# Projecting q and k of an attention and mixture-of-experts layer in three float32r products instead of one float32 product

## Reference: what is computed

```python
qkv = x @ W_qkv                      # (16, 1024, 256) @ (256, 768)
q, k, v = jnp.split(qkv, 3, axis=-1) # 16 heads of 16 each
q, k = _rope(q, k)
att = jnp.einsum('bhtd,bhsd->bhts', q, k) / math.sqrt(DH) + mask
y = jnp.einsum('bhts,bhsd->bhtd', softmax(att), v)
x = layernorm(x + y @ W_o)
x = layernorm(x + mixture_of_experts(x))
```

## Time and profile before

| what | value |
|---|---|
| median of 3 runs | 2942.26 us (2939.76 to 3778.07) |
| the profiled execution, its own time | 2941.85 us |
| span of its trace | 2940.1 us |
| PE busy | 2800.5 us, 95% |
| DVE busy | 2651.2 us, 90% |
| ACT busy | 1782.9 us, 61% |
| GpSimd busy | 1061.1 us, 36% |
| one turn of `mid` | 176.1 us, 14 of them |

### The profile page before, as it was taken

The page is one execution under the profiler, slowest core; times in us unless marked ns, Lnnn a source line. Parts: engine busy times, 40 slices in busy tenths (PEclk is TensorE's granted clock), DMA queues, the critical chain, the costliest instruction groups (busy, mean ns, idle before and its releaser), DMA issues. The chain is left out here.

```text
span 2940.1 us, 58492 instructions
## 1 busy us (share of the span) xinstructions
PE 2800.5 (95%) x18752; PEld 1425.7 (48%) x18752; DVE 2651.2 (90%) x8449; ACT 1782.9 (61%) x4125; POOL 1061.1 (36%) x1295
## 2 busy tenths in 40 slices
PE   5899999999999999999999999999999999999987
PEld 2234545545455554545554455554545555455545
DVE  7899999999999999999899999999999999998855
ACT  1466565666756666575666766666575666756650
POOL 3254333343433434334343423434333343423110
PEclk8799999999999999999999999999999999999998
DMA  3112021120212112021110212112021110212000
GB/s 128 35 49 76 20 80 34 46 58 27 77 34 66 37 41 73 20 81 34 50 54 30 73 34 72 31 41 73 20 81 37 50 51 30 77 30 59 2 30 15
DMA packets 136930, 143.84 MB, mean 49 GB/s; under 512 B 29080, under 2 KB 111280, under 8 KB 136368
## 3 DMA queue, kind: packets, MB, share of 16 engines
q1 hardware_dynamic: 135168, 135.88, 15.3%
q10 hardware_dynamic: 1456, 4.23, 0.4%
HBM read 88.11 MB, written 50.33 MB: 47 GB/s over the span
## 5 line engine op out<-in xcount | busy, mean ns | idle before, releaser
L848 ACT ACTIVATE weights<-bank 128x512 f32<-128x512 f32 (+3 forms) x3072 | 1286.5, 496 | 687.0 <-PE bank L1205 679.0
L977 DVE CUSTOM_DVE_ANT_0 bank<-bank,far_q 128x384 f32<-128x384 f32 (+3 forms) x2048 | 949.6, 520 | 70.0 <-PE bank L1189 56.9
L980 DVE TENSOR_REDUCE maxima<-bank 128x1 f32<-128x512 f32 x1024 | 643.1, 683 | 6.7 <-PE bank L1189 4.7
L1227 PE MATMUL attend<-weights,values 128*32 128x512 f32 (+3 forms) x6144 | 635.6, 499 | 7.4 <-POOL weights L767 5.8
L767 POOL TENSOR_SCALAR_AFFINE_SELECT weights<-weights 128x512 f32<-128x512 f32 x512 | 323.8, 639 | 872.2 <-ACT weights L848 869.9
L1189 PE MATMUL bank<-k_stack,q_stack 48*128 48x512 f16 (+3 forms) x3072 | 511.6, 333 | 41.3 <-DVE maxima L977 12.3
L1205 PE MATMUL bank<-q_stack,k_stack 51*128 51x512 f16 (+3 forms) x3072 | 495.3, 330 | 8.6 <-DMA q_stack<-lowrows 5.4
L1189 PEld LDWEIGHTS bank<-k_stack,q_stack 48*128 48x128 f16 x3072 | 164.0, 94 | 458.8 <-issue 143.7
L1129 PE MATMUL bank<-wexp_hi,zT_hi 128*128 128x512 f32 x1024 | 341.0, 414 | 0.9 <-DVE maxima L977 0.2
L1205 PEld LDWEIGHTS bank<-q_stack,k_stack 51*128 51x128 f16 x3072 | 156.9, 94 | 376.4 <-issue 165.6
L1129 PE MATMUL bank<-wexp_lo,zT_hi 128*128 128x512 f32 x1024 | 319.3, 393 | 0.0
(11 more groups left out here) (115 smaller groups left out, 2909.4 us busy)
## 6 DMA issues: line engine op xcount, KB each, us to landing
parts_scratch<-parts SPq DMA_DIRECT2D x128, 256.0 KB, 2.1
q_stack<-parts_scratch SPq DMA_DIRECT2D x384, 64.0 KB, 2.2
k_stack<-parts_scratch SPq DMA_DIRECT2D x384, 64.0 KB, 2.2
x_in<-in_x SPq DMA_DIRECT2D x64, 256.0 KB, 3.0
z<-in_x SPq DMA_DIRECT2D x32, 512.0 KB, 4.3
out<-z SPq DMA_DIRECT2D x32, 512.0 KB, 2.9
q_stack<-lowrows SPq DMA_DIRECT2D x384, 4.0 KB, 1.7
z<-in_w_exp ACTq DMA_DIRECT2D x1, 1024.0 KB, 4.9
```

Source lines behind the costliest of these rows:

```text
L848: act.activation(weights[:, n % NW, hh, c0:CH], bk[bank(c.seg, step)][:, c0:CH], ACT.Exp, scale=DH ** -0.5).then_inc(S["weights_ready"], 1)
L977: dve.tensor_tensor_reduce(out=b[:, 0:w], in0=b[:, 0:w], in1=far_q[:, CH - w:CH], scale=1.0, scalar=-SENTINEL, op0=ALU.add, op1=ALU.max, a ...
L980: dve.tensor_reduce(dst, b[:, 0:w], AX.X, ALU.max).then_inc(fr, 1)
L1227: last = pe.matmul(pv[32 * j:32 * j + 32, c0:CH], values[:, (s + 1) % SLOTS, o:o + 32], weights[:, n % NW, j, c0:CH], start=kb == 0, stop= ...
```

## The change

`XT` gives three tiles instead of one. ACT copies the bank twice, to `xT` as before and to `xT_hi` in float32r, and raises `x_hi_ready`. DVE then takes the bank less `xT_hi` into `xT_lo` and frees the bank. `QK` waits for both `XT` of its 512 tokens to be freed and runs six float32r matmuls with `split_matmul`, as `MOE` does. Before the first step DVE splits the q and k columns of `wqkv` into `wqk_hi` and `wqk_lo`. The tables and banks stay as they are; each `XT` in them now has a part on DVE.

```diff
+        xT_hi = sb("xT_hi", [P, KT, T], F32R)
+        xT_lo = sb("xT_lo", [P, KT, T], F32R)
+        wqk_hi = sb("wqk_hi", [P, KT, 2 * D], F32R)
+        wqk_lo = sb("wqk_lo", [P, KT, 2 * D], F32R)
...
                 if kind == "XT":
                     (j,) = a
                     filled(act, c, step)
-                    act.activation(xT[:, :, 2 * P * j:2 * P * (j + 1)], b[:, :].rearrange("p (k n) -> p k n", k=KT),
-                                   ACT.Copy).then_inc(fr, 1)
+                    tokens = slice(2 * P * j, 2 * P * (j + 1))
+                    act.activation(xT[:, :, tokens], b[:, :].rearrange("p (k n) -> p k n", k=KT), ACT.Copy)
+                    act.activation(xT_hi[:, :, tokens], b[:, :].rearrange("p (k n) -> p k n", k=KT), ACT.Copy) \
+                       .then_inc(S["x_hi_ready"], 1)
...
             dve.wait_ge(S["w_loaded"], W_LOADS * DMA)
+            dve.tensor_copy(wqk_hi[:, :, :], wqkv[:, :, 0:2 * D]).then_inc(S["wqk_split"], 1)
+            dve.wait_ge(S["wqk_split"], 1)
+            dve.tensor_tensor(wqk_lo[:, :, :], wqkv[:, :, 0:2 * D], wqk_hi[:, :, :].bitcast(F32), ALU.subtract) \
+               .then_inc(S["wqk_split"], 1)
...
-                if kind == "B":
+                if kind == "XT":
+                    (j,) = a
+                    tokens = slice(2 * P * j, 2 * P * (j + 1))
+                    dve.wait_ge(S["x_hi_ready"], c.at("x_hi_ready", step))
+                    dve.tensor_tensor(xT_lo[:, :, tokens], b[:, :].rearrange("p (k n) -> p k n", k=KT),
+                                      xT_hi[:, :, tokens].bitcast(F32), ALU.subtract).then_inc(fr, 1)
+                elif kind == "B":
...
                     if c.seg == "pre" and (s, k) == (0, 0):
                         pe.wait_ge(S["w_loaded"], W_LOADS * DMA)
+                        pe.wait_ge(S["wqk_split"], 2)
+                    emptied(pe, c, ("XT", 2 * ch))
                     emptied(pe, c, ("XT", 2 * ch + 1))
                     room()
                     col = which * D + s * P
-                    for kt in range(KT):
-                        last = pe.matmul(b[:, :], wqkv[:, kt, col:col + P], xT[:, kt, ch * CH:(ch + 1) * CH],
-                                         start=kt == 0, stop=kt == KT - 1)
-                    last.then_inc(fu, 1)
+                    split_matmul(b[:, :], lambda i, kt: (wqk_hi, wqk_lo)[i][:, kt, col:col + P],
+                                 lambda j, kt: (xT_hi, xT_lo)[j][:, kt, ch * CH:(ch + 1) * CH]).then_inc(fu, 1)
```

More of the change, by code:

```diff
@@ L364 @@
     "values_copied": ("VCOPY",), "maxima_ready": ("MC",),
-    "averaged": ("N2",), "rooted": ("R1", "R2"), "normed": ("N1A", "N2A"), "hi_ready": ("ZT",),
+    "averaged": ("N2",), "rooted": ("R1", "R2"), "normed": ("N1A", "N2A"), "hi_ready": ("ZT",), "x_hi_ready": ("XT",),
     "shifted": ("GA",), "gate_exp": ("GA",), "gates_ready": ("GB",),
@@ L583, in attention_moe_kernel @@
         names = [*COUNTED, "link", "parts_ready", "turning", "sines", "sp_waits", "pool_waits", "dve_waits",
-                 "zeroed", "zeroed_v", "stepped", "bias_zeroed", "bias_split", "const_v", "const_p", "ident_ready", "w_loaded", "we_loaded", "hi_split", "w_split"]
+                 "zeroed", "zeroed_v", "stepped", "bias_zeroed", "bias_split", "const_v", "const_p", "ident_ready", "w_loaded", "we_loaded", "hi_split", "w_split", "wqk_split"]
         names += [f"{n}{i}" for n in ("stack", "maxrow") for i in range(SLOTS)]
```

## The result

The changed kernel takes 3013.89 us (median of 4 runs, 3009.77 to 3019.13), the kernel before 2942.48 us beside it: a ratio of 1.0244, with a 95% interval from 1.0229 to 1.026. One execution of the kernel before took 3778.07 us and is a slow one; the ratio goes by the fast ones alone. The change makes the kernel 2.4% slower, 72 us. The forecast was 2998 us, within a range of 2955 to 3020.

A forecast was written before the change was run, and what follows sets the result against it. DVE was taken to bound the kernel where XT stands. A turn costs 2.4 + 1.5 - 0.35 = 3.55 us; 15 of these give 53, with the start 56, added to 2941.85: 2998 us, 1.9% slower, range 2955 to 3020.

The forecast's parts named there:

- DVE sets the pace, QK's saving is mostly without effect: From 1117 to 1182 us of a turn PE follows DVE; QK's 43.5 us saving on PE counts only behind QK.0.3.
- The credit behind QK.0.3: Where DVE idles for PE behind QK.0.3, the shorter QK gains 0.35 us a turn, bounds 0 and 0.40.
- Four subtractions, 2.4 us a turn: DVE's new work at the four XT steps: 0.60 us each, bounds 0.60 and 0.68, 2.4 us a turn.
- DVE's wait for ACT, 1.5 us a turn: At XT, DVE waits until ACT has made both copies: 1.5 us a turn, bounds 0 and 2.7.
- QK.0.0 and HT.0.0 wait for the held banks: PE waits there for the subtractions, but DVE has several finished banks before it by then: cost nothing.
- I expect no change from the clock in the turns: The granted clock, 1.00 in all four stretches of the turn read, was expected to stay at the 2.4 GHz level.
- ACT is hidden: Four more ACT copies at 0.48 us, 1.9 us a turn, cost nothing beyond DVE's wait for them.
- The start, 3 us: Before the turns, the weight split delays XT.0's subtraction, holding its bank and a token load: 3 us, bounds 0 and 5.6.
- the first QK is a little shorter: At the start, the first QK step was expected to be a little shorter; no size of its own given.
- PE as the bound: Rival: QK's saving counts in full and DVE's work is hidden, 2901 us, 1.4% faster; chance 0.08.
- The delay hidden: Rival: DVE's 5.8 us a turn of waits for PE take up the delay, leaving only the start, 2945 us; chance 0.09.
- ACT late: Rival: an exponential precedes ACT's copies at two of four waits, 4.55 us a turn, 3013 us, 2.4% slower; chance 0.11.

The follow-up runs named there:

- the last run: Against the changed kernel, three matmuls ahead of PE's waits are repeated in the turns, 11 more matmuls a turn, to keep PE busy: 2999.08 us, ratio 1.0193.

## Why the prediction was right, and where it was not

The time lay in the range and the direction was the likelier of the two, for most of the reasons given. But a change within 2% was held likelier (0.59) than one slower by more (0.39), and the latter came: the forecast of 2998 was 16 us short.

In the profiled executions the span grew by 68.0 us, where 56 were forecast. Thirteen turns took 58.6 us more (46.2 forecast). The time ahead of them grew by 2.9 us (6.6 forecast) and that behind the last XT.0 by 6.5 (419.6 in place of 413.1; 3.6 forecast), and these two nearly cancel. So the 12 us that the forecast lacks there stand in the turns, 180.5 us in the mean, and they are one step. The median lies 4 us above the profiled execution, in executions of which there is no trace.

*DVE sets the pace, QK's saving is mostly without effect.* Right. With QK in float32 the loss is 9 us more, not 42. The credit behind QK.0.3 was put at 0.35 us a turn; 9 / 15 would be 0.6, but the traces show 0.2 to 0.3 at that place (DVE's wait of 0.19 us, and four reductions in 2.59 us in place of 2.47).

*Four subtractions, 2.4 us a turn.* Right: they run 0.60 us from start to start where two stand together, and doing them twice costs at least as much again.

*DVE's wait for ACT, 1.5 us a turn.* Right in kind and place, a little too high: 1.1 us in the trace, 1.2 by the turns of the kernel with later subtractions. XT.1 came without a wait. The 0.06 us that the working adds for the semaphore stood on no row; in the trace after, the subtraction starts 0.03 us behind ACT's copy (1145.22 + 0.62, then 1145.87).

*QK.0.0 and HT.0.0 wait for the held banks, "so I cost that at nothing".* Right for DVE at an even clock: the turns with a clock of 1.00 cost 3.5 us, the forecast's 3.55, with PE's waits in them. That the two agree so well is partly luck: DVE waits 0.4 us less for ACT than forecast, and a small operation named below takes 0.4 us more.

*"I expect no change from the clock in the turns".* This is the step that failed. I read 1.00 in all four stretches before and took it to stay, while the same text forecast more idle time of PE ahead of XT.1, QK.0.0 and HT.0.0. Behind PE's new gaps the clock fell in ten of thirteen turns. Nine of these are 1.2 us longer than the turns without a fall and one 1.9, together 12.7 us: the 12 us that the profiled execution took beyond the forecast. In the medians the last run got 15 us back.

*ACT is hidden.* Right in the changed kernel; without DVE's part its fourth copy ahead of HT.0.0 shows.

*The start, 3 us.* The mechanism came as described, and then was given back. On the way in, XT.2 of the first sequence went on at 21.84 us (19.06 in the earlier trace rows; forecast 22.3):

```profile
18.30 1.29 DVE L981 TENSOR_TENSOR xT_lo<-bank,xT_hi 128x512 fp32r<-128x512 f32 x2
19.01 0.97 SPq L667 DMA_DIRECT2D x_in<-in_x  x2
21.84 1.97 PE L1173 MATMUL bank<-ident,x_in 128*128 128x128 f32 x8 [13.72 <-DMA x_in<-in_x]
...
26.01 0.74 DVE L1025 STREAM_SHUFFLE rope_swap<-bank 128x512 f32<-128x512 f32 x1
```

The first rotation is late by 2.5 us. Yet ACT's copy of XT.0 in the first segment starts at 126.88, not later than before (127.17). With QK in float32 again that copy is at 129.63, and the 2.5 us stay. So the six matmuls take them back, but by which way is open: their steps are shorter ("the first QK is a little shorter" was one of eight), and with them the clock, low from 45 to 50 us on in all three, also rises earlier. From 104 to 114 us (PE busy, clock, DMA), before, after, and after with QK in float32:

```profile
104.00:114.00 10.00, 9.63 (x52) 0.50 0.01 2
```

```profile
104.00:114.00 10.00, 8.38 (x59) 1.00 0.00 0
```

```profile
104.00:114.00 10.00, 9.63 (x56) 0.50 0.01 2
```

Where the subtraction is left out, the split of the weights is still there and the first rotation is at 23.53 against 23.47 before, so the split is hidden and only the held bank counted.

*The rivals.* PE as the bound: refuted by the float32 run. The delay hidden: DVE's old waits for PE are as long as before, 3.5 and 2.2 us. ACT late: not seen; the time that I gave it, 3013, came by another way.

*Left open.* In this turn a small operation of the gate chain on DVE (L1098) takes 0.64 us beside GpSimd's mask, 0.19 before; it is some 0.4 us a turn, and no run took it apart. Open is also why the clock stays in some turns with the same gaps of PE in front.

## What to carry to other kernels

When a change makes the engine that leads the pace later, look at what it does to PE's clock as well as to PE's waits: PE standing still for under a microsecond several times in a row was free for the schedule and still cost some 15 us through the clock. Compare windows of like length over many turns, and sort them by granted clock before a gap is explained by the wait in front of it. And an operation is not moved to an idle engine for nothing: on GpSimd it was twice as long, and the order of the table, made for another timing, has to move with it.

## What the runs showed of the hardware

The granted clock fell from 2.4 to 1.2 GHz, for 3.4 us, behind four gaps of PE none of which was over 0.95 us. Repeating matmuls that nobody needs made a kernel faster by 0.5%. On DVE the subtraction from SBUF took 685 ns in the mean at its later places, as from a bank (690); at its old place it took 748, some of them up to 1476. On GpSimd it takes 1288 ns. Two float32 matmuls of 128x128 by 128x512 take 1.88 us from start to next start, six float32r matmuls of this shape 1.55.
